# Rolling the 36 written-out slots of a fused transformer stack into a hardware loop of four slots

## The reference, cut to what matters

```python
x = x + L0_xattn(layernorm(x), ctx)    # cross attention over 257 context rows per sequence
x = x + L0_attn(layernorm(x))          # causal self attention, one head of 128
x = x + L0_ffn(layernorm(x))           # 256 -> 1024 -> 256, activations and weights quantised
x = x + L1_xattn(layernorm(x), ctx)    # cross attention, 16 heads of 16
x = x + L1_attn(layernorm(x))          # local attention, window of 2 to each side
x = x + L1_moe(layernorm(x))           # 8 experts, 2 per position, 256 -> 1024 -> 256
```

## Time and profile before

| | |
|---|---|
| median of three executions | 1929.2 us |
| the profiled execution's own time | 1929.94 us |
| its span, first to last instruction | 1928.1 us |
| PE matmul busy | 1752.2 us, 91% |
| PE weight loads busy | 1437.5 us, 75% |
| DVE, ACT, POOL busy | 56%, 44%, 33% |
| DMA | 235.3 MB, 122 GB/s on average |

### The profile page before, as it was taken

One profiled execution on the slowest core, in us unless ns is written; L12 is line 12 of the kernel. 1 busy time (PEld: TensorE's weight loads), 2 busy tenths in 40 slices (PEclk: granted clock), 3 DMA queues, 4 the chain that ended last, 5 costly groups with the idle time before them and its releaser, 6 DMA issues. The chain is left out here.

```text
span 1928.1 us, 37634 instructions
## 1 busy us (share of the span) xinstructions
PE 1752.2 (91%) x12680; PEld 1437.5 (75%) x12713; DVE 1071.5 (56%) x3790; ACT 856.5 (44%) x2361; POOL 642.5 (33%) x1186
## 2 busy tenths in 40 slices
PE   3799999999999999999999999973699999999990
PEld 2477777777777777777777777762699999999990
DVE  4567776777677777777776777747111111111115
ACT  0466665666666666666665666631111111111110
POOL 0234433433343334433443443320233333333320
PEclk7899999999999999999999999995799999999995
DMA  9622222233233233222222220006545545545547
GB/s 309 234 75 83 84 86 80 86 91 89 67 95 91 81 74 92 86 80 83 83 86 80 84 84 18 12 6 236 188 174 183 188 171 185 187 170 187 185 142 267
DMA packets 124351, 235.30 MB, mean 122 GB/s; under 512 B 14448, under 2 KB 76400, under 8 KB 114096
## 3 DMA queue, kind: packets, MB, share of 16 engines
q1 hardware_dynamic: 117392, 214.87, 34.6%
q0 software_dynamic: 6816, 18.62, 2.6%
HBM read 203.16 MB, written 30.28 MB: 121 GB/s over the span
## 5 line engine op out<-in xcount | busy, mean ns | idle before, releaser
L691 ACT ACTIVATE x_prob<-ps,x_nmax 128x257 f32<-128x257 f32 x512 | 238.9, 472 | 228.1 <-DVE x_nmax L992 227.7
L1379 ACT ACTIVATE heT<-ps 128x512 f32<-128x512 f32 x142 | 84.8, 597 | 441.3 <-PE ps L1345 378.1
L1345 PEld LDWEIGHTS ps<-xeT,w_block 128*128 128x128 f32 x2272 | 266.7, 193 | 11.7 <-issue 7.4
L1345 PE MATMUL ps<-xeT,w_block 128*128 128x128 f32 x2272 | 267.3, 276 | 7.5 <-DMA w_block<-in_m_w 7.0
L413 PE MATMUL ps<-context,x_probT 128*128 128x128 f32 x2048 | 272.4, 276 | 0.9 <-ACT x_probT L685 0.8
L413 PEld LDWEIGHTS ps<-context,x_probT 128*128 128x128 f32 x2048 | 256.1, 192 | 9.6 <-DVE x_own L980 1.0
L1331 PE MATMUL ps<-w,heT 128*128 x1136 | 256.8, 379 | 0.0
L1331 PEld LDWEIGHTS ps<-w,heT 128*128 128x128 f32 x1136 | 210.4, 190 | 25.7
L992 DVE TENSOR_REDUCE x_nmax<-ps 128x1 f32<-128x257 f32 x512 | 191.9, 415 | 35.8 <-PE ps L578 35.8
L756 POOL TENSOR_TENSOR x_lastv<-context,x_prob 128x128 f32<-128x128 f32 x256 | 120.1, 469 | 228.9 <-ACT x_prob L691 228.9
L685 ACT ACTIVATE x_probT<-ps 128x512 f32<-128x512 f32 x224 | 133.8, 597 | 124.7 <-PE ps L572 121.8
(11 more groups left out here) (269 smaller groups left out, 3131.9 us busy)
## 6 DMA issues: line engine op xcount, KB each, us to landing
w_block<-in_m_w SPq DMA_DIRECT2D x71, 1024.0 KB
context<-in_cT SPq DMA_DIRECT2D x128, 257.0 KB, 3.0
context<-in_cn SPq DMA_DIRECT2D x128, 256.0 KB, 3.3
context<-in_lastk SPq DMA_DIRECT2D x128, 128.0 KB, 3.6
yrows<-zero SPq DMA_DIRECT2D x1, 8192.0 KB, 28.1
w<-in_m_w SPq DMA_DIRECT2D x8, 1024.0 KB, 11.8
w<-yrows SPq DMA_DIRECT2D x16, 512.0 KB, 6.3
xin<-in_x SPq DMA_DIRECT2D x32, 128.0 KB, 3.3
```

The source lines that it names most:

```text
L691: A(p1[kk % 2][:, g, :], ps[:, g, 0:KEYS], ACT.Exp, bias=nmax1[kk % 2][:, g:g + 1], accum_out=rsum1[kk % 2][:, g:g + 1]).then_inc(e1_ok.ha ...
L1345: t = mm(ps[:, 2 * b + n, f * P:(f + 1) * P], w1[b][:, k, lo:lo + P], xeT[b][:, k, :], start=k == 0, stop=k == H - 1)
L1379: A(heT[b][:, n * FK // 2:(n + 1) * FK // 2, :].rearrange("p k t -> p (k t)"), ps[:, 2 * b + n, :], ACT.Gelu).then_inc(heT_ok.handle, 1)
```

## The change

The slots that are alike are no longer written out 28 times. `slots(eng, work)` writes slots -3 to 0, then one loop body of four slots (so that buffer numbers stay constants), which the hardware loop `eng.Fori` passes (32 - 4) / 4 = 7 times for slots 1 to 28, and then slots 29 to 32. Tile numbers within the body are `Number(register, scale, offset)`, and every semaphore threshold and DRAM address that depends on them is worked out in the engine's registers when it is needed (`known`). SP's loop has 6 passes over four slots, for slots 1 to 24.

```diff
+class Number:
+    def __init__(self, register, scale, offset):
+        self.register, self.scale, self.offset = register, scale, offset
+    def __add__(self, n):
+        return Number(self.register, self.scale, self.offset + n)
+    def __mul__(self, n):
+        return Number(self.register, self.scale * n, self.offset * n)
+
+def known(n):
+    return n.register * n.scale + n.offset if isinstance(n, Number) else n
...
     def W(eng, s, r, k):
-        eng.wait_ge(s.handle, s.at(r, k))
+        eng.wait_ge(s.handle, known(s.at(r, k)))
...
-    def slots(work):
-        for s in range(-3, tiles + 1):
-            work(Slot(s))
+    def slots(eng, work):
+        for s in range(-3, 1):
+            work(Slot(s, s, False))
+        with eng.Fori(0, (tiles - RING) // RING) as i:
+            for c in range(RING):
+                work(Slot(Number(i, RING, 1 + c), 1 + c, True))
+        for s in range(tiles - RING + 1, tiles + 1):
+            work(Slot(s, s, False))
...
-                sp.dma_start(xin[m][:], t_in["x"][t]).then_inc(x_in[m], 16)
+                sp.dma_start(xin[m][:], t_in["x"][known(t)]).then_inc(x_in[m], 16)
...
-            for s in range(tiles + 1):
-                slot(Slot(s))
+            slot(Slot(0, 0, False))
+            loops = tiles // RING - 2
+            if loops > 0:
+                with sp.Fori(0, loops) as i:
+                    for c in range(RING):
+                        slot(Slot(Number(i, RING, 1 + c), 1 + c, True))
+            for s in range(loops * RING + 1, tiles + 1):
+                slot(Slot(s, s, False))
```

More of the change, by code:

```diff
@@ L121, in at, with __sub__ @@
         return tile * len(self.names) + self.names.index(name) + 1
+class Number:
[3 more added lines that the diff above has]
+        return Number(self.register, self.scale, self.offset + n)
+    def __sub__(self, n):
+        return self + -n
+    def __mul__(self, n):
+        return Number(self.register, self.scale * n, self.offset * n)
+def known(n):
+    return n.register * n.scale + n.offset if isinstance(n, Number) else n
 PARTS = {"cross0": 3, "self0": 2, "ffn": 1, "self1": -1}
@@ L283, in stack_phase, with __init__ @@
     class Slot:
-        def __init__(self, s):
-            self.s = s
+        def __init__(self, s, fixed, whole):
+            self.s, self.fixed, self.whole = s, fixed, whole
         def tile(self, ahead):
-            t = self.s + ahead
-            return (t, t % RING) if 0 <= t < tiles else None
+            if not self.whole and not 0 <= self.s + ahead < tiles:
+                return None
+            return self.s + ahead, (self.fixed + ahead) % RING
         def half(self, k):
@@ L335, in load_x @@
             def load_x(t, m):
-                sp.dma_start(xin[m][:], t_in["x"][t]).then_inc(x_in[m], 16)
-                sp.dma_start(lastq[m][:], t_in["lastq"][t]).then_inc(x_in[m], 16)
+                sp.dma_start(xin[m][:], t_in["x"][known(t)]).then_inc(x_in[m], 16)
+                sp.dma_start(lastq[m][:], t_in["lastq"][known(t)]).then_inc(x_in[m], 16)
             def load_batch(t, m, b):
-                sp.dma_start(cT[m][:, b], t_in["cT"][t, :, b]).then_inc(c_in[m], 16)
-                sp.dma_start(cn[m][:, b], t_in["cn"][t, :, b]).then_inc(c_in[m], 16)
-                sp.dma_start(lastk[m][:, b, :], t_in["lastk"][t, b].partition_broadcast(P)).then_inc(c_in[m], 16)
+                sp.dma_start(cT[m][:, b], t_in["cT"][known(t), :, b]).then_inc(c_in[m], 16)
+                sp.dma_start(cn[m][:, b], t_in["cn"][known(t), :, b]).then_inc(c_in[m], 16)
+                sp.dma_start(lastk[m][:, b, :], t_in["lastk"][known(t), b].partition_broadcast(P)).then_inc(c_in[m], 16)
             def slot(sl):
@@ L354, in slot @@
                         W(sp, dve_s["self1"], done[0], "x5")
-                        sp.dma_start(xres[done[0]], x5[done[1] % 2][:]).then_inc(x_saved[done[1] % 2], 16)
+                        sp.dma_start(xres[known(done[0])], x5[done[1] % 2][:]).then_inc(x_saved[done[1] % 2], 16)
                         W(sp, dve_s["router"], done[0], "norm")
-                        sp.dma_start(xnorm[done[0]], xn5[done[1] % 2][:]).then_inc(n_saved[done[1] % 2], 16)
+                        sp.dma_start(xnorm[known(done[0])], xn5[done[1] % 2][:]).then_inc(n_saved[done[1] % 2], 16)
                     if b < NB - 1 and here and after:
@@ L435, in step @@
                         W(pe, act_s["cross0"], t, "q")
-                        pe.wait_ge(c_in[m], (t - m) * (NB * 3 * 16 // RING) + NB * 3 * 16)
+                        pe.wait_ge(c_in[m], known((t - m) * (NB * 3 * 16 // RING) + NB * 3 * 16))
                     for b in range(part * NB // 2, (part + 1) * NB // 2):
@@ L611, in slot @@
                         unit_values(*last)
-            slots(slot)
+            slots(pe, slot)
         @block.scalar
@@ L692, in slot @@
                     sl.steps(table, 2 * k + 1)
-            slots(slot)
+            slots(act, slot)
         @block.gpsimd
@@ L716, in c0_norm @@
                 inverse_std("cross0", t)
-                pool.wait_ge(x_in[m], (t - m) * (32 // RING) + 32)
+                pool.wait_ge(x_in[m], known((t - m) * (32 // RING) + 32))
                 plus_bias("cross0", t, xb["cross0"], xin[m], "x0_bv")
@@ L762, in slot @@
                     sl.steps(table, 2 * k + 1)
-            slots(slot)
+            slots(pool, slot)
         @block.vector
@@ L846, in c0_moments @@
             def c0_moments(t, m):
-                dve.wait_ge(x_in[m], (t - m) * (32 // RING) + 32)
+                dve.wait_ge(x_in[m], known((t - m) * (32 // RING) + 32))
                 moments("cross0", t, xin[m][:])
@@ L951, in s1_x5 @@
                 W(dve, pool_s["self1"], t, "x_bias")
-                dve.wait_ge(x_saved[q], (t - q) * 8 + 16)
+                dve.wait_ge(x_saved[q], known((t - q) * 8 + 16))
                 v_.scalar_tensor_tensor(x5[q][:], bank["self1"][:, 0:D], rinv["self1"][:], xb["self1"][:], ALU.mult, ALU.add).then_inc(dve_s["self1"].handle, 1)
@@ L957, in ro_norm @@
             def ro_norm(t, m):
-                dve.wait_ge(n_saved[m % 2], (t - m % 2) * 8 + 16)
+                dve.wait_ge(n_saved[m % 2], known((t - m % 2) * 8 + 16))
                 normalise("router", t, x5[m % 2][:], xn5[m % 2][:])
@@ L962, in ro_logits @@
                 W(dve, pe_s["router"], t, "logits")
-                v_.tensor_copy(logits[:, t, :], bank["router"][:, 0:EXP]).then_inc(dve_s["router"].handle, 1)
+                v_.tensor_copy(logits[:, known(t), :], bank["router"][:, 0:EXP]).then_inc(dve_s["router"].handle, 1)
             table = {
@@ L1014, in slot @@
                     sl.steps(table, 2 * k + 1)
-            slots(slot)
+            slots(dve, slot)
 def expert_phase(nc, t_in, const, logits, ps, xres, xnorm, yrows, out, tiles, cap, blocks, sem, sig, sb):
```

## The result

| | before | after |
|---|---|---|
| median | 1929.51 us (1927.67 to 1929.94, 4 runs) | 1964.74 us (1962.65 to 1965.19, 4 runs) |
| ratio | | 1.0182, 95% interval 1.0165 to 1.0200 |
| the profiled execution's own time (its span) | 1929.94 (1928.1) us | 1961.54 (1959.7) us |

The loop makes the kernel 35.2 us slower. The forecast was 1949 (1930 to 1980). The direction and the main mechanism were right, the size was 16 us short.

A forecast was written before the change was run, and what follows sets the result against it. The prediction took PE's pace to bound the stack phase, with DVE three quarters full beside it. It summed 1929.9 + 6 (waits) + 14 (code fetched at jumps), less 0.7, to 1949 us, range 1930 to 1980.

The forecast's parts named there:

- The base: Whole kernel before: the profiled execution took 1929.9 us, the median is 1929.2, so 0.7 comes off the sum.
- Registers ahead of single waits 0: Loop slots: register arithmetic ahead of instructions with one wait is hidden by the instruction ahead, 0 us (bounds 0 to 95).
- changed carriers +6: Instructions with two waits, one now on a register instruction: one late DVE wait felt per slot, 28 x 0.21 = +6 us.
- The jump itself 0: End of each pass: compare and branch, 208 ns on PE and 56 on DVE, are hidden, 0 us.
- The code is fetched again: At each of six jumps back PE and DVE wait for their target's code; instruction packets stay near 80; +14 us.
- 3.0 us for the fetch, 0.7 us of cover, 2.3 us of gap: PE at each jump back: code load 3.0 us, partly covered by queued matmuls, PE 2.3 us late; 6 x 2.3 = 14 us.
- The clock left out of the forecast: Behind the six jumps: the forecast's sum had no term for a lower PE clock; only rival B did.
- rival B: Behind each jump: the stall also costs the clock, 6.9 us at half speed; +44 us, 1973 us (far end 1991); chance 0.19.
- ACT and POOL hardly matter: At the jumps: ACT (370 instructions a pass) and POOL (217) hardly stall; the sum stays 14 us.
- Rival A: At the jumps: the code is kept, only the 6 us of waits are left; 1935 us, +0.3%; chance 0.24.
- C: PE's `unit_values` and transposes after a fold: late wait now on the matmul, -11 us, 1918 us, faster; chance 0.08.
- A pass of the expert loop: PE's expert phase: a pass has 104 matmuls and 104 loads, is one instruction packet, and jumping back costs nothing.

The follow-up runs named there:

- e1: Kernel after with all 28 slots written out, no jump back, but thresholds and addresses still worked out from a register holding 0: 1931.87 us, ratio 1.0009.
- e3: Kernel after with the loop on PE only; DVE, ACT and POOL written out with constants, no hint: 1957.53 us, ratio 1.0141.
- e6: Kernel after with the loop kept on ACT and POOL only; PE and DVE written out: 1940.64 us, ratio 1.0050.
- e9: Kernel after with a prefetch hint in the loops of PE, ACT, POOL and SP, and DVE written out: 1930.39 us, ratio 1.0000.
- e7: Kernel after plus a prefetch hint for the branch back at the top of each pass, on all five engines: 1934.68 us, ratio 1.0026.
- e8: Kernel after with the loop on PE only, with prefetch hint; DVE, ACT and POOL written out with constants: 1929.74 us, ratio 1.0002.
- e2: Kernel after with a loop body of eight slots passed three times, so two jumps back in place of six: 1940.03 us, ratio 1.0055.
- e4: Kernel after with PE's slots written out with constants; DVE, ACT and POOL keep the loop, no hint: 1953.68 us, ratio 1.0134.

## Why the prediction was right or wrong

- *The base* holds.
- *Registers ahead of single waits 0, changed carriers +6.* Together 2.3 us (interval 0 to 3.5) in e1. The value for the carriers was too high, the direction right. The parts of PE, ACT and POOL are nothing: the slots without a jump last 38.1 us, as before, in e3, in e6 and in e9, and 38.2 in the kernels in which DVE works with registers. So the cost is DVE's.
- *The jump itself 0.* Right: with the hint the same jumps leave no gap on PE.
- *The code is fetched again.* Right, and it is the cause, shown by e7 and e8. The packets (91, forecast near 80) and the idle times at six slot ends stand where the prediction put them.
- *3.0 us for the fetch, 0.7 us of cover, 2.3 us of gap.* The gap was 18.7/6 = 3.1 us, from two errors of opposite sign. The taken branch lasts 4.3 to 5.0 us on PE, not 3.0: I had priced it as a plain load. But PE's sequencer reaches it 1.8 us before the matmuls it has issued are done, where I had read 0.7 from the timeline. Term: 18.7 in place of 14.
- *The clock left out of the forecast.* This is the step that was missed, and most of the 16 us. I had made it rival B, at 0.19, since 2.3 us lay between the two rows I had. The gaps were 2.8 to 3.5 us, and the clock fell behind all six: 10.8 us. B itself took a fetch of 3.6 us for each jump, that is 2.9 us of idle, and 6.9 us at half speed, 44 us in all with the waits' 6; five of six had 3.4 us at half speed. Forecast and B each had half of it right.
- *ACT and POOL hardly matter.* Wrong for ACT by itself (e6, +10.6 us): as executed its pass has 446 instructions, not 370, and it waits for them. On the sum it has little effect, since ACT's stall lies beside PE's: the profiled execution with PE's loop alone is 29.4 us slower than before, the one with all loops 31.6, and the difference is the size of the registers' 2.3.
- *Rival A (code kept) and C (faster) fall.* PE's better carriers at `unit_values` did not show as a gain beyond 0.1 us per pass.
- *A pass of the expert loop* executes 100 matmuls and 100 loads, not 104 each. Nothing hangs on it.

Terms as measured: 18.7 + 10.8 + 2.3 = 31.8 us, where the profiled execution is 31.6 slower. That execution was 3.2 us faster than the median of the others, and the rest of the 35.2 us lies in those. Its mean granted clock is 0.955, theirs 0.952 to 0.954, so they spent more time at the lower level. Whether that was behind the jumps is not shown, since only one execution was traced. That forecast and result lie within 16 us of each other is in part luck: the fetch and its cover were both taken too short, and the carriers too dear by 4 us, which makes up for a part of what was left out.

## What to carry to other kernels

A hardware loop whose body an engine can't keep costs that engine a wait for code at each jump back, some 3 us of idle time here, and 4.4 to 6.0 us for a jump with the clock behind it. Count executed instructions per pass and engine, and look at the length of the taken branch on PE and at "issue" idle behind the branch on the others. A prefetch hint at the head of the pass takes the wait away nearly completely; then see to it that no engine leaves the loop into a stretch where nothing covers one late fetch.

## What the runs showed of the hardware that was not expected

- The same gap does not always bring the lower clock. 3.12 us (e3, first jump) and 3.10 us (e2, second jump) left it at 1.00, while 2.79 and 2.93 us (the kernel after) were followed by 3.4 us at 0.50. In the kernel where only ACT and POOL loop, a gap of 1.94 us was followed by 6.8 us at half speed and one of 2.08 by none. The length of one gap alone does not decide.
- A taken branch to code that is gone lasts 4.3 to 5.8 us on PE. On DVE the branch itself is 63 ns and the next instruction comes 2.8 to 4.0 us later; on ACT the branch is 45 ns and the engine is idle for some 3 us behind it (e4 and e6).
- What an engine keeps: POOL 217 instructions but not 439 (e2), PE 1440 but not 1820; ACT does not keep 446, nor DVE 788.
- With the hint PE's branch lasts 333 ns, against 208 in the expert loop.
- Three engines stalled separately cost 28 and 24 us; together 35.
